# Linear attention in a two-layer fused kernel: state summed over normalised tokens, values folded in once per batch

## The reference, cut to what matters

```python
x = layernorm(x)                                   # 8 x 1024 x 256, no gain or shift
q, k, v = split(einsum('bnd,ed->bne', x, W_qkv))   # each 256 wide
q = relu(q) + 1e-6
k = relu(k) + 1e-6
kv = einsum('bnd,bne->bde', k, v)                  # one 256 x 256 state per batch
z = 1 / (einsum('bnd,bd->bn', q, k.sum(axis=1)) + 1e-6)
attn = einsum('bnd,bde,bn->bne', q, kv, z)
out = attn @ W_out.T + b_out                       # then layernorm and residual
```

## Time and profile before

| | us |
|---|---|
| median of 3 runs | 1897.93 |
| lowest, highest | 1897.42, 1899.61 |
| profiled execution, first to last instruction (span) | 1900.1 |
| TensorE busy | 1843.4 |
| VectorE busy | 1496.8 |
| ScalarE busy | 1069.6 |
| GpSimd busy | 624.2 |

### The profile page before, as it was taken

The page is one execution under the profiler, slowest core; times in us unless marked ns, Lnnn a source line. Parts: engine busy times, 40 slices in busy tenths (PEclk is TensorE's granted clock), DMA queues, the critical chain, the costliest instruction groups (busy, mean ns, idle before and its releaser), DMA issues.

```text
span 1900.1 us, 31592 instructions
## 1 busy us (share of the span) xinstructions
PE 1843.4 (97%) x11542; PEld 1631.5 (86%) x11542; DVE 1496.8 (79%) x3901; ACT 1069.6 (56%) x1734; POOL 624.2 (33%) x927
## 2 busy tenths in 40 slices
PE   8999999999999999999899999999999999999996
PEld 7888878888888888888779998888988799999996
DVE  7777579999999999999748884789998566666663
ACT  5656725566566665666456663665564255555552
POOL 3211001234433333444604443134534312333333
PEclk9999999999999999999899999999999899999998
DMA  5545242222222221201143422134322312222210
GB/s 178 163 150 167 81 153 68 90 86 95 89 84 83 94 82 64 78 26 37 51 152 124 134 87 89 60 119 135 100 89 76 90 60 82 93 83 86 76 51 18
DMA packets 132610, 176.95 MB, mean 93 GB/s; under 512 B 11486, under 2 KB 115813, under 8 KB 132328
## 3 DMA queue, kind: packets, MB, share of 16 engines
q1 hardware_dynamic: 121704, 159.87, 26.3%
q0 software_dynamic: 10752, 15.06, 2.3%
HBM read 113.25 MB, written 76.51 MB: 100 GB/s over the span
## 4 chain that ended last, share of the span: by engine, by line
PE 86%; DVE 5%; ACT 2%; POOL 2%; DMA 2%; issue 2%; SPq 0%; POOLq 0%; DVEq 0%; ACTq 0%
PE ps L385 78%; PE ps L409 4%; PE ps L712 2%; PE ps L701 1%; POOL d_p L2587 1%; DVE bst L1614 1%; PE ps L470 1%; DMA stage<-in_w 0%; DMA stage<-in_wi 0%; DVE rO L2155 0%; DMA xa<-in_x 0%; DVE wslotA L1820 0%; DMA d_x<-df 0%; DVE pay L1939 0%; DVE kl L1639 0%
## 5 line engine op out<-in xcount | busy, mean ns | idle before, releaser
L385 PE MATMUL ps<-wslotA,fh 128*128 128x256 f32 x1776 | 326.1, 284 | 0.0
L1830 DVE TENSOR_TENSOR fl<-fF,fh 128x512 fp32r<-128x512 f32 x316 | 214.0, 683 | 94.2 <-ACT fF L1209 93.3
L385 PEld LDWEIGHTS ps<-wslotA,fh 128*128 128x128 f32 x1776 | 280.4, 191 | 5.2 <-DVE fl L1830 0.2
L385 PE MATMUL ps<-wslotA,fl 128*128 128x256 f32 x888 | 251.2, 283 | 0.0
L2582 POOL TENSOR_TENSOR smalls<-smalls,powers 128x4 f32<-128x4 f32 x87 | 28.0, 321 | 591.7 <-DVE smalls L1617 591.6
L2587 POOL DMA_INDIRECT d_p<-pay,sut x128 | 154.3, 1205 | 103.7 <-DVE pay L1987 57.4
L385 PE MATMUL ps<-x2h,wslotA 128*128 128x512 f32 x512 | 171.0, 396 | 0.2 <-DVE x2l L1639 0.2
L385 PEld LDWEIGHTS ps<-wslotA,fl 128*128 128x128 f32 x888 | 170.0, 191 | 0.0
L1208 ACT ACTIVATE fh<-ps,b1e 128x512 fp32r<-128x512 f32 x126 | 86.9, 690 | 143.0 <-PE ps L385 140.6
L385 PE MATMUL ps<-wslotB,fh 128*128 128x256 f32 x752 | 137.1, 283 | 0.4 <-DVE fl L1830 0.4
L385 PE MATMUL ps<-eh,wslotB 128*128 128x512 f32 x384 | 125.3, 393 | 2.4 <-DVE el L2011 2.4
(11 more groups left out here) (383 smaller groups left out, 5146.5 us busy)
## 6 DMA issues: line engine op xcount, KB each, us to landing
stage<-in_w SPq DMA_DIRECT2D x16, 1024.0 KB, 5.6
d_p<-blank SPq DMA_DIRECT2D x24, 528.0 KB, 4.8
pay<-d_p SPq DMA_DIRECT2D x24, 528.0 KB, 3.7
d_x<-df SPq DMA_DIRECT2D x16, 516.0 KB, 3.5
xA<-d_x SPq DMA_DIRECT2D x16, 516.0 KB, 3.7
xa<-in_x SPq DMA_DIRECT2D x16, 512.0 KB, 4.9
d_h<-hh SPq DMA_DIRECT2D x16, 512.0 KB, 5.4
d_h<-hl SPq DMA_DIRECT2D x16, 512.0 KB, 3.0
```

What stands on the lines that cost most here:

```text
L385: return pe.matmul(o, a, b, start=start, stop=stop, skip_group_check=True)
L1830: ve.tensor_tensor(dl[:, half(k)], df_[:, half(k)], f32(dh[:, half(k)]), ALU.subtract).then_inc(S["low"], 1)
```

## The change: what it does

By algebra, sum(k v^T) = sum(k (x W)^T) = sum(k x^T) W, where x is the normalised token and W the folded value weights. The new kernel sums the 256x256 product of normalised tokens `u` (not transposed, split into `uh`, `ul`) and keys in `acc`, and multiplies it once per batch by W in a new call `state_values`, whose result `KW` lies in a tile of the ring. Since the mean of a normalised token is zero, column 255 is the negative sum of the others: the weights are replaced by differences to their row 255 (`weights_differences` on VectorE), and column 255 of `xnA` holds ones, which gives the sum of the keys and carries the 1e-6 into queries and keys. The feature map becomes Relu on ScalarE (high part, straight from PSUM) and one VectorE instruction max(ps, 1e-6) - high (low part), also straight from PSUM.

The core of it:

```diff
             def keys(g, k):
...
-                    t = three(ps[:, half(i % 2)], [(xAh[g % 2][:, q[c]], xAl[g % 2][:, q[c]], wq_h[:, c, 256:768],
-                                                    wq_l[:, c, 256:768]) for c in range(2)], True, True)
+                    t = three(ps[:, i % 2 * 256:i % 2 * 256 + 256],
+                              [(xAh[g % 2][:, q[c]], xAl[g % 2][:, q[c]], wq_h[:, c, 256:512], wq_l[:, c, 256:512])
+                               for c in range(2)], i % 2 == 0, True)
             def state(g, k):
+                evacuated("K", g, k)
...
+                        t = three(acc[:, half(c, 256)], [(uh[g % 2][:, q], ul[g % 2][:, q], hv[:, i, :], lv[:, i, :])],
+                                  first, end)
+            def state_values(bt):
+                pe.wait_ge(S["stl"], bt + 1)
...
+                ps = unit("KW", bt)
+                for m in range(2):
+                    q = slice(m * 128, m * 128 + 128)
+                    t = three(ps[:, half(m, 258)], [(st_h_[:, c, q], st_l_[:, c, q], wx_h[:, c, :], wx_l[:, c, :])
+                                                    for c in range(2)], True, True)
+            def q_high(g):
+                act.activation(qh[g % 3], ring.of("Q", g).ap, ACT.Relu).then_inc(S["qh"], 1)
+            def k_high(g, k):
+                    act.wait_ge(S["sta"], 2 * (g - 1) + k + 1)
+                act.wait_ge(S["k"], 2 * g + k + 1)
+                act.activation(kk_h[:, half(k)], ring.of("K", g, k).ap[:, 0:512], ACT.Relu).then_inc(S["ksh"], 1)
+            def u_high(g):
+                if g >= 2:
+                    act.wait_ge(S["sta"], 2 * (g - 1))
+                copy(uh[g % 2], xnA).then_inc(S["xn_l"], 1)
+            def xl_norm(g):
+                    act.wait_ge(S["ul"], g)
+            def q_low(g):
+                ve.scalar_tensor_tensor(ql[g % 3], u.ap, 1e-6, f32(qh[g % 3]), ALU.max, ALU.subtract).then_inc(u.free, 1)
+            def k_low(g, k):
+                ve.scalar_tensor_tensor(kk_l[:, half(k)], u.ap[:, 0:512], 1e-6, f32(kk_h[:, half(k)]), ALU.max,
+                                        ALU.subtract).then_inc(u.free, 1)
+            def u_low(g):
+                ve.tensor_tensor(ul[g % 2], xnA, f32(uh[g % 2]), ALU.subtract).then_inc(S["ul"], 1)
```

More of the change, by code:

```diff
@@ L265, in build @@
         xAl = [tile("xAl0", 4, R), tile("xAl1", 8, R)]
[L266 to L269, removed]
+        kk_h, kk_l = tile("kk_h", 6, R), tile("kk_l", 7, R)
+        uh = [tile("uh0", 9, R), tile("uh1", 11, R)]
+        ul = [tile("ul0", 10, R), tile("ul1", 12, R)]
+        stt = tile("stt", 13, R)
+        st_h_, st_l_ = v3(stt[:, 0:512], 2, 256), v3(stt[:, 512:1024], 2, 256)
+        wqk_v, wlast = v3(stage[:, 0:1024], 2, 512), stage[:, 1024:1536]
         wv_v = v3(stage[:, 1536:2048], 2, 256)
@@ L1022, in tensor_program @@
                     xl_t(2 * s + 3)
+            state_values(7)
             prefix(1, 12)
@@ L1329, in values_folded @@
             def values_folded():
                 act.wait_ge(S["vw"], 1)
[L1331 removed]
+                copy(wx_h[:, 0, 256:258], blank[:, 0:2])
+                copy(wx_h[:, 1, 256:258], ident[:, 127:128].to_broadcast([128, 2]))
+                copy(wx_h[:, :, 0:256], two(ring.of("VW").ap)).then_inc(S["vwh"], 1)
                 act.wait_ge(S["w1"], 8 * (G + E))
[L1333 to L1335 removed]
+                for i in range(4):
+                    copy(xv(xnA)[:, i, 255:256], ones[:, 0:1])
@@ L1569, in scalar_program @@
                     xl_norm(2 * s + 3)
-                    v_copy(2 * s + 2, 0)
+                    k_high(2 * s + 2, 0)
                 if s in PAIRS:
-                    kw_high(s)
+                    state_high(s)
                 if s + 1 in PAIRS:
                     xl_high(2 * s + 3)
-                    kv_high(2 * s + 2, 0)
+                    u_high(2 * s + 3)
                 if s - 1 in PAIRS:
@@ L2459, in vector_program @@
                 if s in PAIRS:
-                    q_relu(2 * s)
+                    q_low(2 * s)
                 if s == 1:
@@ L2471, in vector_program @@
                 if s in PAIRS:
-                    q_low(2 * s)
-                    k_relu(2 * s, 1)
+                    k_low(2 * s, 1)
                 if s - 1 in PAIRS:
@@ L2492, in vector_program @@
                 if s in PAIRS:
-                    kv_low(2 * s + 1, 0)
-                    k_relu(2 * s + 1, 1)
+                    k_low(2 * s + 1, 0)
                 if s - 1 in PAIRS:
@@ L2499, in vector_program @@
                 if s in PAIRS:
-                    q_relu(2 * s + 1)
-                    kv_low(2 * s + 1, 1)
+                    k_low(2 * s + 1, 1)
                     q_low(2 * s + 1)
                 if s + 1 in PAIRS:
-                    k_relu(2 * s + 2, 0)
+                    u_low(2 * s + 2)
                 if s - 2 in PAIRS:
@@ L2511, in vector_program @@
                 if s in PAIRS:
-                    kw_low(s)
+                    state_low(s)
                 if s + 1 in PAIRS:
+                    k_low(2 * s + 2, 0)
                     lows(xAl[(2 * s + 3) % 2], xAh[(2 * s + 3) % 2], ring.of("XLT", 2 * s + 3), S["xlh"], 2 * s + 3)
+                    u_low(2 * s + 3)
             for n in range(E - 1, 3 * E):
```

193 lines of the change are left out of this document (97 added, 96 removed).

## The result

The changed kernel took 1921.33 us (median of 4 runs, 1917.67 to 1922.38), the kernel before 1897.68 us on the same chip (4 runs, 1895.9 to 1899.61): a ratio of 1.0121, with the interval 1.0106 to 1.0135. It is 1.2% slower. The forecast, 1908 us, had the direction and less than half of the size (+10 us, measured +23.7 between the medians); the time lies 1.3 us above the range. The profiled execution took 1922.38 us, with a span of 1920.6 us against 1900.1. These 20.5 us are what the traces can account for; the other 3 are not placed, since the span of the kernel before already lies 2.2 us above the median of its runs.

A forecast was written before the change was run, and what follows sets the result against it. TensorE bounds, VectorE close behind, but ring waits lengthen pairs. Expert 7 +2.35, first pairs -6.9, four pairs +14.4, after pair 6 -0.1: +9.8 us, 1908 us on the median; range 1894 to 1920.

The forecast's parts named there:

- the first pairs: Pairs 0 to 2, from xl_t(0) to xl_t(7): 6.9 us shorter, between 10 and 3 shorter.
- the last rival: Key matmuls: they don't get cheaper at half the columns; chance 0.02.
- The ring's four waits: TensorE in each pair waits for PSUM tiles freed late by k_low or q_low: 2.6, 1.1, 2.9, 0.8 us.
- the walk: One pair followed turn by turn through the ring of three PSUM tiles: 39.4 us against 35.8.
- the row against the rule: Row: a 4.6 us wait brought half rate. Rule: frequent brief idling moves the clock back and forth. The forecast followed the row.
- The third rival: The clock falls in every pair, costing 2.7 to 3 us each, five pairs: +15, 1923 us; chance 0.12.
- None of that loss, 2.7 us: Pair 2, behind the weight load: idle 3.6 for 4.6 us, so the earlier half-rate loss would not recur.
- wait 1: In a pair, keys(2s+1,1) waits for k_low(2s+1,0), which stands behind route1 and so the logits: 2.6 us.
- Expert 7: Last expert before attention: weights_differences and weight splits delay the last lows and w2_end: +2.35 us (0 to 3).
- After pair 6: Pair 7 and its attention output: two waits fall away, state work stands ahead: -0.1 us (-2 to +3).
- TensorE stays fed: VectorE reaches each k_low before TensorE needs the tile, so the sums decide: -26.7 us, 1871; chance 0.12.
- Only part of the waits: VectorE reaches state_low early, the wait before xl_t(2s+3) falls away: pair 36.4 us, total 1896; chance 0.12.

The follow-up runs named there:

- e9_two_xn: The kernel of e8_weights_later with two copies of the normalised tokens xnA instead of one; 1877.23 us, ratio 0.9879.
- e1_k_first: Changed kernel with k_high(2s+1,0) moved ahead of xl_high and k_low(2s+1,0) ahead of stats_o, lows and route1; 1903.71 us, ratio 1.0027.
- e2_k_before_state: Changed kernel with k_low(2s+2,0) moved on VectorE ahead of route1, stats_5th and state_low; 1907.13 us, ratio 1.0054.
- e6_reordered: Changed kernel with the moves of e1_k_first, e2_k_before_state and e4_expert7, plus q_high, t_turned, k_high and u_low moved earlier; 1887.56 us, ratio 0.9947.
- e5_fill_both: Changed kernel with unread matmuls in both long waits of a pair: 18 ahead of keys(2s+1,1), 23 ahead of xl_t(2s+3); 1915.29 us, ratio 1.0089.
- e8_weights_later: The kernel of e6_reordered with the weight splits of pairs 1 and 2 moved ahead of q_high(2s+1) and q_low(2s+1); 1880.48 us, ratio 0.9903.
- e4_expert7: Changed kernel with weights_differences and the QKV weight splits moved behind the last low of expert 7; 1915.35 us, ratio 1.009.
- e3_fill: Changed kernel with 18 unread matmuls ahead of keys(2s+1,1), in the first long wait of a pair; 1921.62 us, ratio 1.0118.
- e7_before_late: Kernel before the change with k_relu(2s+1,0) moved behind route1 and v_copy(2s+1,0) behind xl_high; 1928.29 us, ratio 1.0154.

## Why the prediction was right in direction and wrong in size

The profiles differ by 20.4 us over the four stretches, where the sum said 9.8. Two terms make the miss in nearly equal parts: pairs 3 to 6 by 5.7 us and the first pairs by 5.9. In both it was mainly the clock that the prediction had wrong.

- **What bounds the kernel, and the sums.** Right in kind; the work was put a little low. By the prediction's own row three matmuls of 258 columns take 0.37 us, so a call of 12 takes 1.48 and not 1.45, and TensorE's own work in a pair 32.0 and not 31.85 us. Measured it is some 32.3: e9_two_xn runs a pair in 33.2 with 0.9 us of waits. (VectorE's 33.01 less 3.8 is 29.2 and not 30.3; the changed kernel's pair has 29.37.) Keys of 256 columns run at 0.12 us a matmul (timeline after, twelve in 1.50), so the last rival is out.
- **The price of max-then-subtract.** Right: taken as 1.15 for 1024 columns, measured 1.14 from start to start; taken as 0.62 for 512, measured 0.60.
- **The ring's four waits.** Right in place, cause and nearly in size: 2.6, 1.1, 2.9, 0.8 forecast; 2.3, 0.9, 2.9, 0.9 measured. e1_k_first and e2_k_before_state each take one away alone, e6_reordered nearly all of them. At full clock (e5_fill_both) the pair takes 39.3 us, where the walk ended at 39.4. That this is so close is in part luck: 0.4 us too much waiting stood against 0.4 too little work.
- **The clock in pairs 3 to 6.** This step failed. The walk ran TensorE at full rate behind every wait; the paragraph on the clock set the row against the rule and decided "by the row, whose wait was longer, it stays". That one row, a fall behind an idle time of 4.6 us, says that such a wait lowers the clock; it does not say that a shorter one doesn't, and I took it so. The kernel before even had the contrary in it: its wait of 1.9 us, the second of the earlier trace rows, ends at 1465.77 and half clock follows, with TensorE less than fully busy ahead of it (13.41 of 17.00 us); TensorE alone, 3 us:

```profile
1467.00:1470.00 3.00, 3.00 (x16) 0.52 0.09 25
```

  The changed kernel's trace agrees with the rule instead ("TensorE: Matmul & The Clock Gate", section "A second HAM failure mode: psum-queue depth-cycling", of the Trainium skill): the clock goes back and forth in each pair, 0.96 on average. The third rival, "the clock falls in every pair", was thus the right mechanism with too dear a price: 2.7 to 3 us a fall, read from a stretch of 6 us at half rate, where about 3.4 us at half rate cost 1.5. With that added to the walk's 39.4, four pairs come to +20.4 against the forecast +14.4; +20.1 was measured.
- **The first pairs.** This step failed too: -6.9 forecast, -1.0 measured, outside its own bounds (-10 to -3). "None of that loss, 2.7 us" was the wrong term: the clock did not stay up, but fell three times. Windows of TensorE alone behind xl_t(1), behind the weight load of pair 2 and behind its wait 1, and the waits of the changed kernel, 1180 to 1287 us:

```profile
1186.00:1188.00 2.00, 1.87 (x10) 0.72 0.40 73
1188.00:1190.00 2.00, 2.00 (x6) 0.50 0.59 200
...
1256.00:1258.00 2.00, 2.00 (x11) 0.50 0.78 255
...
1270.00:1272.00 2.00, 2.00 (x11) 0.50 0.49 161
```

```profile
PE ps L389 <- DVE small L2181: 4.9, 2, 2.7
PE ps L389 <- DVE kk_l L2150: 4.6, 3, 2.3
PE ps L413 <- ACT xnA L1091: 3.2, 2, 1.9
PE ps L389 <- DVE ql L2145: 1.8, 2, 0.9
PE ps L389 <- DVE xAl L1667: 1.6, 1, 1.6
```

  These are 16.1 us of waits; the kernel before has 8.2 in the same stretch. That "most ring waits are missing" was right for pairs 0 and 1: only 6.4 us of them stand behind k_low and q_low, nearly all in pair 2, and the rest behind loads and tokens. What failed can be followed from xl_t(0) on. xl_t(1) came where it was walked and then ran at 0.50; the end of pair 0, xl_t(3), came 1.6 us earlier than before where 3.65 were forecast, so 2.0 late. The second weight load took 9.65 us in place of 8.66, and the first attention output of pair 2 came 3.6 us earlier for the forecast 6.5: another 0.9. From there to xl_t(7) the kernel before took 30.45 us and the changed one 33.03, where the forecast had it 0.4 us shorter than before: another 3.0, with two falls of the clock. That is the 5.9 us: 0.9 at the load and 5.0 where the clock fell. As an estimate from the granted clock, each fall was some 3.4 us at half rate and so cost up to 1.7 us, 5.1 for the three. No run holds the clock up in these pairs, so this split is read from one trace and not shown by an experiment. What is shown is that the order matters here as well: e1_k_first alone brings 5.9 us, and moving the weight splits (e8_weights_later) 6.5.
- **Expert 7.** Right: +2.35 forecast, +2.3 measured, and gone when the instructions are moved (e4_expert7).
- **After pair 6.** -0.1 forecast, -1.0 measured, inside its bounds.
- **The rivals.** "TensorE stays fed" would have been 1871 us. It did not happen with this order, but its arithmetic was sound: e9_two_xn comes to 1877 once VectorE reaches each release in time and the splits have moved. "Only part of the waits" did not happen.
- **The range.** It closed at 1920 because the clock rival was added to the forecast's middle with a chance of 0.12. The median lies between the forecast and that rival.

## What to carry to other kernels

When an evacuation that only copied is folded into the operation that uses the data, the PSUM tile is now freed at that operation's place in its engine's list: walk the ring's turns against that list, and move the releases forward before judging the arithmetic by its time. Here the order was worth 7 us in a pair of 41, where the arithmetic took 3.5 us of work from TensorE (35.8 to 32.3). And price every new TensorE wait twice, once for itself and once for the matmuls that run at half rate behind it; look up every wait of the old trace for this, the short ones too, and not only the longest.

## What the runs showed of the hardware

- An idle time of 2.3 us behind transpositions and matmuls of 8 columns was followed by half clock in the changed kernel's pairs, and one of 2.9 us behind full matmuls, in the same pair, was not. With the first wait filled (e3_fill) or gone (e1_k_first) the second one lowered the clock. A wait's length alone did not decide, and unread matmuls helped only where both waits had them.
- A fall in pairs 3 to 6 cost 1.5 us: 40.8 against 39.3 us a pair (e5_fill_both); in e1_k_first pairs of 38.2 to 38.5 us stand beside one of 36.9 without it.
- The price of a fall isn't fixed: one wait of 2.8 us a pair made the kernel before 5.2 us a pair slower (e7_before_late), 2.4 us beyond the wait itself, at a granted clock of 0.92 over a pair, where the changed kernel has 0.96. The half rate lasted about 5 us behind the wait there, for 3.4.
